# A four-layer graph network: the adjacency load reordered, its degree sums made by one-column products, and the first two layer-0 blocks interleaved

## What is computed

```python
h = jnp.maximum(_layernorm(x, axis=-1), 0.0)
# layer 0, with graph = adj
gt = graph.T
deg = jnp.sum(gt, axis=1)              # column sums of adj
d_inv_sqrt = deg ** (-0.5)
norm = d_inv_sqrt[:, None] * gt * d_inv_sqrt[None, :]
x = x + norm @ (h @ weight) + bias
```

## Time and profile before

| what | value |
|---|---|
| three runs | 840.29 us median (839.44 to 842.71) |
| the profiled execution | 845.75 us, of which the span is 843.6 us |
| PE busy | 765.0 us, 91% of the span |
| DVE busy | 645.4 us, 77% |
| ACT busy | 394.7 us, 47% |
| mean granted TensorE clock | 0.978 of 2.4 GHz |

### The profile page before, as it was taken

One profiled execution on the slowest core, in us unless ns is written; L12 is line 12 of the kernel. 1 busy time (PEld: TensorE's weight loads), 2 busy tenths in 40 slices (PEclk: granted clock), 3 DMA queues, 4 the chain that ended last, 5 costly groups with the idle time before them and its releaser, 6 DMA issues.

```text
span 843.6 us, 18563 instructions
## 1 busy us (share of the span) xinstructions
PE 765.0 (91%) x6597; PEld 639.5 (76%) x6597; DVE 645.4 (77%) x1370; ACT 394.7 (47%) x756; POOL 51.5 (6%) x76
## 2 busy tenths in 40 slices
PE   0667599788999999987979999999999999999898
PEld 0334388677999999973458888888888888888687
DVE  4788688376877777754689999999999999997011
ACT  1566500014555555524555555575557555754300
POOL 1000111010110011110000000000000000000000
PEclk9999899988999999997999999999999999999999
DMA  6477300204898888741940135113611282112395
GB/s 230 160 253 267 118 2 0 99 25 150 299 300 287 284 285 285 241 137 45 226 130 1 26 92 159 26 27 76 175 27 26 66 266 95 26 27 76 152 358 188
DMA packets 96661, 120.45 MB, mean 143 GB/s; under 512 B 3488, under 2 KB 82016, under 8 KB 92384
## 3 DMA queue, kind: packets, MB, share of 16 engines
q1 hardware_dynamic: 94448, 111.85, 40.5%
q0 software_dynamic: 2160, 7.87, 4.8%
HBM read 76.15 MB, written 35.68 MB: 133 GB/s over the span
## 4 chain that ended last, share of the span: by engine, by line
PE 71%; issue 13%; DVE 8%; SPq 3%; DMA 2%; ACT 1%; POOL 1%; DVEq 0%; POOLq 0%; ACTq 0%
PE ps L677 13%; PE ps L679 13%; PE ps L678 13%; PE ps L567 3%; PE ps L547 3%; PE ps L569 3%; PE ps L572 3%; PE ps L570 3%; PE ps L568 3%; PE ps L718 3%; PE ps L719 3%; SPq L352 2%; DVE arena L1100 1%; SPq L364 1%; DMA row_pair<-in_L_gnn_bias_dram 1%
## 5 line engine op out<-in xcount | busy, mean ns | idle before, releaser
L677 PE MATMUL ps<-arena 128*128 128x257 f16 x1024 | 280.6, 274 | 2.9 <-DVE arena L1280 2.9
L679 PE MATMUL ps<-arena 128*128 128x257 f16 x1024 | 280.0, 273 | 0.0
L678 PE MATMUL ps<-arena 128*128 128x257 f16 x1024 | 279.8, 273 | 0.0
L951 ACT ACTIVATE arena<-arena 128x512 f16<-128x512 f32 x252 | 158.6, 629 | 137.9 <-PE ps L679 137.4
L1265 DVE SCALAR_TENSOR_TENSOR arena<-arena,w_j 128x512 f32<-128x512 f32 x256 | 190.0, 743 | 0.9 <-DMA arena<-exp_adj_t 0.9
L1270 DVE TENSOR_TENSOR arena<-arena 128x512 f16<-128x512 f32 x256 | 176.3, 689 | 7.6 <-ACT arena L951 7.3
L677 PEld LDWEIGHTS ps<-arena 128*128 128x128 f16 x1024 | 100.1, 98 | 16.2 <-DVE arena L1280 3.4
L678 PEld LDWEIGHTS ps<-arena 128*128 128x128 f16 x1024 | 100.6, 98 | 12.7
L679 PEld LDWEIGHTS ps<-arena 128*128 128x128 f16 x1024 | 100.0, 98 | 13.2
L523 PE MATMUL ps<-arena 128*128 128x256 f16 x256 | 72.4, 283 | 13.7 <-DVE arena L1079 8.1
L1155 DVE SCALAR_TENSOR_TENSOR arena<-ps,arena 128x512 f16<-128x512 f32 x64 | 44.0, 688 | 39.6 <-ACT arena L818 39.4
(11 more groups left out here) (137 smaller groups left out, 1035.6 us busy)
## 6 DMA issues: line engine op xcount, KB each, us to landing
arena<-in_adj_dram SPq DMA_DIRECT2D x64, 512.0 KB, 4.8
adj_t_parts<-arena SPq DMA_DIRECT2D x16, 1024.0 KB, 4.3
exp_adj_t<-arena SPq DMA_DIRECT2D x16, 1024.0 KB, 7.1
arena<-exp_adj_t SPq DMA_DIRECT2D x64, 256.0 KB, 4.2
arena<-adj_t_parts SPq DMA_DIRECT2D x16, 1024.0 KB, 7.5
x<-arena POOLq DMA_DIRECT2D x15, 512.0 KB, 4.8
arena<-u_rows SPq DMA_DIRECT2D x4, 1024.0 KB, 14.9
x<-in_x_dram SPq DMA_DIRECT2D x1, 2048.0 KB, 8.4
```

The lines of the kernel that those rows point to most:

```text
L677: mm(ps[:, bank, 0:DE], hi, ht_hi[:, head, j, 0:DE], start=s, stop=False)
L678: mm(ps[:, bank, 0:DE], hi, ht_lo[:, head, j, 0:DE], start=False, stop=False)
L679: ins = mm(ps[:, bank, 0:DE], lo, ht_hi[:, head, j, 0:DE], start=False, stop=e)
L951: nc.scalar.activation(p_hi[:, j % 4, :], prob[:, j % 4, :], copy).then_inc(p_hi_done, 1)
```

## The change

What it does, part by part:

- SP issues half 0 and 1 of `adj` first, then `x` in four pieces of four row blocks, w0, and more halves between them; w3 and the bias come after half 9. `stage` has 5 slots. The loops of the load phase are written out over 32 halves.
- DVE makes the statistics of `x` in four pieces at halves 1, 3, 6 and 10, POOL `rstd` in four pieces. The sign of w3 moves to half 16, its transposes to half 17, PSUM bank 5.
- The layernorm's relu moves from DVE to ACT (`h0_relu`, scale `rstd`, bias `neg_shift`); DVE only copies to float16 and subtracts.
- Row block t of `x` goes with half `row_slot(t)` = 5 + (3t)//2: 5, 6, 8, 9, 11, 12 and so on. Its parts are made and transposed at that half, copied and multiplied at the next one, the result copied at the one after that.
- Degrees: for each half 8 column blocks x 2 parts, `nat` is now the stationary side and one column of ones the moving one. The sum comes out with one column sum on each partition, so the 16 diagonal reads go, and one scaling of 128x16 takes their place.
- POOL makes `dinv_in` in four pieces (1, 3, 5 and 7 columns) and ACT begins with the first; `dinv_out` comes after `g_lo`.
- After the last degree product PE runs ten products of 512 columns whose result nothing reads.
- Layer-0 blocks 0 and 1 are made together, six products for each j.
- The first loads of the second pass wait for the end of the first pass.

```diff
         def _(sp):
-            sp.dma_start(x[:, :, :], x_rows).then_inc(x_in, 16)
...
+            load_half(0)
+            load_half(1)
+            load_x(0)
+            load_half(2)
             sp.dma_start(w0_f, w0_d.rearrange("(c p) d -> p c d", p=P)).then_inc(w0_in, 16)
...
+            load_half(3)
+            load_x(1)
+            load_half(4)
+            load_x(2)
+            for n in range(SLOTS, HALVES):
+                sp.wait_ge(nat_lo_done, n - SLOTS + 1)
+                load_half(n)
+                if n == SLOTS + 2:
+                    load_x(3)
+                if n == SLOTS + 4:
+                    sp.dma_start(w3_f, w3_d.rearrange("(c p) d -> p c d", p=P)).then_inc(w3_in, 16)
+                    sp.dma_start(bias, b0_d.partition_broadcast(P)).then_inc(w3_in, 16)
...
         def _(pool):
+            for p in range(4):
+                pool.wait_ge(stats_done, p + 1)
+                nc.gpsimd.tensor_tensor(rstd[:, XP * p:XP * p + XP], var_eps[:, XP * p:XP * p + XP],
+                                        neg_half[:, XP * p:XP * p + XP], ALU.pow).then_inc(rstd_done, 1)
             pool.wait_ge(deg_copied, 1)
+            for lo, hi in DINV_PIECES:
+                nc.gpsimd.tensor_tensor(dinv_in[:, lo:hi], deg[:, lo:hi], neg_half[:, lo:hi], ALU.pow
+                                        ).then_inc(dinv_done, 1)
...
         def _(pe):
+            def degrees(n):
+                j, s = n // 2, n % 2
+                pe.wait_ge(nat_lo_done, n + 1)
+                for a in range(s * HBK, (s + 1) * HBK):
                     for part in range(2):
-                        ins = mm(ps[:, 4 + q, :].rearrange("p (a n) -> p a n", a=4), ones16[:, :],
-                                 nat[:, 4 * q:4 * q + 4, part, j, :],
-                                 start=(first and part == 0), stop=(last and part == 1))
+                        ins = mm(ps[:, 4, a:a + 1], nat[:, a, part, j, :], ones16[:, 0:1], start=False,
+                                 stop=(j == NB - 1 and part == 1), skip_group_check=True)
...
+            mm(ps[:, 4, 0:NB], ones16[:, :], zero16[:, :], start=True, stop=False, skip_group_check=True)
+            for n in range(HALVES):
+                ins = degrees(n)
+                for t in range(NB):
+                    if row_slot(t) == n:
+                        h0_transposes(t)
+                    if row_slot(t) + 1 == n:
+                        h0_products(t)
+                if n == SLOTS + 12:
+                    turn_w3()
+            ins.then_inc(deg_done, 1)
+            for k in range(10):
+                mm(ps[:, 5, :], ones16[:, :], nat[:, 0, 0, 0:4, :], start=True, stop=True)
...
+            for j in range(NB):
+                pe.wait_ge(g_lo_done, j + 1)
+                s, e = (j == 0), (j == NB - 1)
+                for b in range(2):
+                    mm(ps[:, 2 + b, 0:D], nat[:, b, 0, j, :], g_hi[:, j, :], start=s, stop=False)
+                    mm(ps[:, 2 + b, 0:D], nat[:, b, 0, j, :], g_lo[:, j, :], start=False, stop=False)
+                    ins = mm(ps[:, 2 + b, 0:D], nat[:, b, 1, j, :], g_hi[:, j, :], start=False, stop=e)
...
         def _(act):
+            for n in range(HALVES):
+                adj_high(n)
+                if n == 2:
+                    act.wait_ge(w0_in, 16)
+                    nc.scalar.activation(w0_hi, w0_f, copy, scale=W_SCALE).then_inc(w0_hi_done, 1)
+                for t in range(NB):
+                    if row_slot(t) + 2 == n:
+                        hw_copy(t)
+                    if row_slot(t) + 1 == n:
+                        h0_turned(t)
+                    if row_slot(t) - 1 == n:
+                        h0_relu(t)
+                if n == SLOTS + 14:
+                    act.wait_ge(w3_t_ps, 1)
...
         def _(dve):
+            for n in range(HALVES):
+                adj_low(n)
+                if n in (1, 3, 6, 10):
+                    x_stats((1, 3, 6, 10).index(n))
+                if n in (3, 5, 8, 12):
+                    x_shift((3, 5, 8, 12).index(n))
+                if n == 4:
+                    dve.wait_ge(w0_hi_done, 1)
+                    v.scalar_tensor_tensor(w0_lo, w0_f, W_SCALE, w0_hi, ALU.mult, ALU.subtract
+                                           ).then_inc(w0_lo_done, 1)
+                if n == SLOTS + 11:
+                    sign_w3()
+                for t in range(NB):
+                    if row_slot(t) == n:
+                        h0_parts(t)
 
             dve.wait_ge(deg_done, 1)
-            for t in range(NB):
-                ins = v.tensor_tensor_reduce(junk[:, t % JUNK, :], ps[:, 4 + t // 4, (t % 4) * P:(t % 4 + 1) * P],
-                                             ident[:, :], 1.0, 0.0, ALU.mult, ALU.add, deg[:, t:t + 1])
...
+            v.tensor_scalar(deg[:, :], ps[:, 4, 0:NB], 2.0 ** -16, None, ALU.mult).then_inc(deg_copied, 1)
```

More of the change, by code:

```diff
@@ L185, in ps16 @@
             return ps[:, bank, :].bitcast(F16)
-        x_in = sem("x_in")
+        x_in = [sem(f"x_in{p}") for p in range(4)]
         w0_in = sem("w0_in")
+        w3_in = sem("w3_in")
         w2_in = sem("w2_in")
@@ L192, in gnn_stack @@
         ident_zero = sem("ident_zero")
+        slot_in = [sem(f"slot_in{k}") for k in range(SLOTS)]
         half_in = [sem(f"half_in{k}") for k in range(4)]
@@ L292, in _, with load_half, load_x @@
         def _(sp):
-            sp.dma_start(x[:, :, :], x_rows).then_inc(x_in, 16)
-            sp.dma_start(w0_f, w0_d.rearrange("(c p) d -> p c d", p=P)).then_inc(w0_in, 16)
[L295 to L310, removed]
+            def load_half(n):
+                sp.dma_start(stage[:, n % SLOTS, :], adj_rows[n // 2][:, (n % 2) * HALF:(n % 2 + 1) * HALF]
+                             ).then_inc(slot_in[n % SLOTS], 16)
+            def load_x(p):
+                sp.dma_start(x[:, XP * p:XP * p + XP, :], x_rows[:, XP * p:XP * p + XP, :]).then_inc(x_in[p], 16)
+            load_half(0)
+            load_half(1)
+            load_x(0)
+            load_half(2)
+            sp.dma_start(w0_f, w0_d.rearrange("(c p) d -> p c d", p=P)).then_inc(w0_in, 16)
+            load_half(3)
[10 more added lines that the diff above has]
+                    sp.dma_start(bias, b0_d.partition_broadcast(P)).then_inc(w3_in, 16)
             def load_pass2(i, b, first):
@@ L480, in h0_transposes, with h0_products @@
                 ins.then_inc(h0_t_ps, 1)
-            def h0_products(t, b, first):
+            def h0_products(t):
+                b = t % 2
                 pe.wait_ge(h0_t_done, t + 1)
-                if not first:
+                if t == 0:
+                    pe.wait_ge(w0_lo_done, 1)
+                if t >= 2:
                     pe.wait_ge(hw_done, t - 1)
@@ L744, in _, with adj_high @@
             copy = ACT.Copy
[L746 to L753, removed]
+            def adj_high(n):
+                j, s = n // 2, n % 2
+                act.wait_ge(slot_in[n % SLOTS], 16 * (n // SLOTS + 1))
@@ L754, in adj_high, with h0_relu @@
                 nc.scalar.activation(nat[:, s * HBK:(s + 1) * HBK, 0, j, :],
-                                     stage[:, k, :].rearrange("p (a n) -> p a n", a=HBK), copy,
+                                     stage[:, n % SLOTS, :].rearrange("p (a n) -> p a n", a=HBK), copy,
                                      scale=ADJ_SCALE).then_inc(nat_hi_done, 1)
-            def h0_turned(t, b, first):
+            def h0_relu(t):
+                if t % XP == 0:
+                    act.wait_ge(shift_done, t // XP + 1)
+                    act.wait_ge(rstd_done, t // XP + 1)
+                if t >= 2:
+                    act.wait_ge(h0_lo_done, t - 1)
+                nc.scalar.activation(hrelu[:, t % 2, :], x[:, t, :], ACT.Relu, bias=neg_shift[:, t:t + 1],
+                                     scale=rstd[:, t:t + 1]).then_inc(relu0, 1)
@@ L767, in hw_copy @@
+            def hw_copy(t):
                 act.wait_ge(hw_ps, t + 1)
-                nc.scalar.activation(hw[:, t, :], ps[:, 2 + b, 0:D], copy,
+                nc.scalar.activation(hw[:, t, :], ps[:, 2 + t % 2, 0:D], copy,
                                      scale=1.0 / (H_SCALE * W_SCALE)).then_inc(hw_done, 1)
[L771 to L779, removed]
@@ L792, in _ @@
             for t in range(NB):
+                for piece, (lo, hi) in enumerate(DINV_PIECES):
+                    if t == lo:
+                        act.wait_ge(dinv_done, piece + 1)
                 nc.scalar.activation(g_hi[:, t, :], hw[:, t, :], copy,
@@ L1006, in _, with sign_w3 @@
-            for t in range(NB):
[L1007 to L1016, removed]
+            def sign_w3():
+                dve.wait_ge(w3_in, 32)
+                link(v.tensor_scalar(w3_s, w3_f, 0.0, None, ALU.is_lt))
+                v.scalar_tensor_tensor(w3_s, w3_f, 0.0, w3_s, ALU.is_gt, ALU.subtract).then_inc(w3_signed, 1)
@@ new lines, in x_stats @@
+            def x_stats(p):
+                dve.wait_ge(x_in[p], 16)
```

(8 more changed lines are left out.)

149 lines of the change are left out of this document (50 added, 99 removed).

## The result

| | before | changed |
|---|---|---|
| median | 842.71 us (5 runs, 839.44 to 843.68) | 834.22 us (5 runs, 833.47 to 835.37) |
| ratio | | 0.992, 95% interval 0.9892 to 0.9948 |
| profiled execution | 845.75 us, span 843.6 | 834.22 us, span 832.3 |

A second set of runs gave 833.65 against 842.45, ratio 0.9904 (0.9871 to 0.9936). The ratio is the recorded one, with its interval; the two medians divide to 0.990.

What follows compares the result with a forecast made beforehand. It took a chain of waits through the load to DVE's end of `g_lo` as the bound. POOL's start 10.3 us sooner, `g_lo` 1.1 quicker and DVE delayed 0.5 gave 10.9 off 840.3: 829.4 us, range 818 to 844.

Steps and rivals of the forecast that it cites:

- the sum: Load terms at half rate to POOL's start at 84.7, plus what follows: total gain 10.9, taken off the median 840.3.
- The likeliest case: PE at half clock rate through the load: 829.4 us, chance 0.40.
- What bounds the kernel: Chain through load and degrees to DVE's end of `g_lo`, on which layer 0 hangs; no engine is full.
- One for one: A shift of DVE's end of `g_lo` shifts the kernel's end equally; nothing later absorbs it.
- The start: Beginning of the load: first ACT conversion near 4.5, PE starting at 13, DVE ending half 5 at 18.6.
- The steady part: Load cycle of three halves for two row blocks: 7.7 us at half rate, 6.6 at full, against 5.9 before.
- Half rate: PE's clock at half in the load, having no stretch as dense as before: 829.4 us, chance 0.40.
- The tail: Behind the load: POOL starts at 84.7 against 95.00, then `g_lo` with `dinv_out` gains 1.1 us.
- delay DVE 0.5: If PE comes cold from the load, the unread products run into the first `g_lo` and delay DVE 0.5 us.
- 4.3 and 10.5: PE's times behind the load: ten unread products 4.3 us at half rate, two layer-0 blocks 10.5 at full.
- Costed at nothing: Second-pass loads, five slots, w3's sign, statistics piece 3 and, beyond halves 2 to 6, queued `x` pieces: no cost.
- the rivals: Half-rate load 829.4 (0.40), full rate 821.5 (0.33), no chain 811 (0.05), nothing 843.4 (0.12), slower, 851 (0.10).

Runs made afterwards that it cites:

- later twice: Changed kernel with ACT's copy of the transposes and PE's products one half later, the copy of the result two halves later: 820.1 us.
- later: Changed kernel with ACT's copy of the transposes, PE's products and the copy of the result each one half later: 833.3 us.
- blocks in turn: Changed kernel with layer-0 blocks 0 and 1 made one after the other, as before the change: 832.72 us.
- fillers: Changed kernel with unread 512-column products added where PE idles in the load's cycle of three halves: 827.77 us.
- the tail alone, written out: Kernel before with only the new degrees, scaling, POOL's pieces and unread products, and PE's load loop written out: 833.58 us.

## Why the prediction came out

Forecast 829.4 in 818 to 844, gain 10.9; measured 834.22, gain 8.5 in the medians. Of the 4.8 us between forecast and measured time 2.4 are in the start of the sum: it was taken off a median of three runs, 840.3, where five gave 842.71. The likeliest case was the one that happened.

- **What bounds the kernel** held, but not to the microsecond. The moment DVE has its first block passes to the end: 9.2 us sooner there, 8.5 in the median. From the first add to the end of the span all fourteen traces have 728 to 734 us, so large shifts arrive (14.2 us sooner in "later twice", 13.6 in the medians, those on two chips), while the 2.3 and 2.4 us of "later" and "blocks in turn" did not show in the median as such. "One for one" was more than these runs bear out. In the profiled pair the gain was 11.3, because POOL's gap before its next power was 9.59 instead of 10.53 us in that execution, among other things; across the runs here that gap is 7.0 to 10.6 us and follows nothing that was changed.
- **The start** held: first conversion expected near 4.5, seen 4.84; half 5 expected to end at 18.6, seen 19.45; PE expected at 13, seen 12.5.
- **The steady part** held in mechanism and in sum: 7.7 expected, 7.6 seen. Of its terms, the one-column products at half rate were 0.58 for 16 (0.64 taken), the relu 0.49 to ACT's next operation (0.41 taken from the scaled copy), the six products 1.23 from their start to the transposes' (1.28). The runs with fillers (6.7, expected 6.6 at full rate) and "later twice" confirm clock and chain apart. Half rate was given only 0.40; nothing in the trace before decided it, so that this case came is in part luck. Why the clock stays down here (but for a few us about 51 and 82) was not settled, only what it costs: 7.6 against 6.7 a cycle. Narrow products start 0.028 us apart. That is close to the 25 ns that the Trainium skill gives in "TensorE: Matmul & The Clock Gate", "Back-to-back issue gap". By an estimate from the 107 ns that the Trainium skill gives for a load of 128 columns in "TensorE: Matmul & The Clock Gate", "LDWEIGHTS", 16 of them would have taken 1.7 us if each had waited for its load. The trace agrees with it as a duration, since a load lasts 104 ns at the median; but the loads overlap, and for the spacing the measured 0.58 decides.
- **The tail**: POOL's start 84.7 expected, 85.29 seen. The mis-sized term is what follows. The first add should have come at 84.7 + 9.2 + 4.1 + 0.5 = 98.5 and came at 100.26. `g_lo` was 1.1 us quicker than taken (2.2 instead of 1.1 saved, with `dinv_out`), but the "delay DVE 0.5" measured 2.76: PE was tied up by unread products until 89.1 and needed 11.2 more until the first block was there, both being made together and the first eight products not yet at full rate. I had 4.3 and 10.5 and never set their sum against DVE's time with an early `g_lo`. The two errors cancel in part. At the first add they leave a gain of 9.2 instead of 10.9; "blocks in turn" shows the wait gone there, though not its whole worth in the median.
- **Costed at nothing**: second-pass loads and five slots showed no wait, and `x` in the queue none beyond the early halves where the sum had it (ACT's waits for DMA in the load, 8.3 us, are all in the first 18 us). The unread products, which I took to save a cold start, save nothing measurable.
- **Not seen at all**: the order of the loads, which looks like the change's main part (20 us earlier at the start), is for the most part eaten by its own chain. Beside the tail alone, written out, the change ends the load 3.7 us sooner (84.36 against 88.07), has 1.4 of it at the first add, behind PE's 2.76 us, and nothing in the medians. The new order with the old tail was not run. And the rivals did not hold the best variant: with the copies moved, ACT's work is the bound, at 5.7 a cycle.

## What to carry to other kernels

In a pipeline of engines whose order is written by hand, lay out one cycle as a chain of waits and look for a step that asks in the next slot for what another engine makes in this one. Giving it two slots was worth some 13 us here, giving it to only one of two such steps next to nothing. A gain at the start is spent again if the steady rate drops; compare the cycle before with the cycle after before counting the start. Many very small products with addresses from a loop's counter are worth a try in straight-line code: here that decided between no gain and 10 us.

## What the runs showed of the hardware

- One-column products, each with its own 128x128 weight load, took 0.58 us for 16 at half rate and 0.55 at full: the clock hardly matters to them. Six products of 256 columns took 1.44 and 0.81.
- With addresses made from a loop register they start 0.086 us apart instead of 0.028 (2.84 against 1.04 us for 32).
- The granted-clock column says 1.00 until after 50 us in the changed kernel, while six products take 1.44 us there from 21.8 on; in "later" it says 1.00 through the whole load, where all groups of six take 1.44 or 1.46. The duration of a known product tells the clock; in these traces the column shows a low clock only behind the first fall.
- POOL stood 9.6 to 10.9 us before its first select in every trace, whether `x` or `adj` was being loaded, and 7.0 to 10.6 us before its first power behind the maximum.
